# New tables of step places for a token tower followed by attention and MLP on one core

## What is computed

```
x = embed[tokens] + PE
for i in range(2):
    h = ln(x);  q, k, v = h@wq, h@wk/4, h@wv             # 8 heads of 16
    k, v = causal_conv(basis, k), causal_conv(basis, v)  # along the 256 positions
    Z = v (x) k;  g = relu(Z.gate_k + gate_b)**2 + 1e-5
    o = q . cumsum(g*Z) / (cumsum(g) + 1e-5);  o = o / max(|o|, 1e-5)
    x = x + o@wo;   x = x + gelu(ln(x)@ff1)@ff2
h = ln(x)@out_k + out_b                                   # 256 wide
h = h + attn(layernorm(h))    # 16 heads of 64: q (k^T v) / 8, then W_o; no softmax
h = h + mlp(layernorm(h))     # (silu(x@gate) * (x@up)) @ down, hidden 768, int8-valued weights / 127
```

## Time and profile before

| | |
|---|---|
| median of the runs | 1988.42 us |
| the profiled execution, its own time | 1988.27 us, 2.2 us of it outside the span |
| its span, first to last instruction | 1986.1 us |
| mean granted TensorE clock | 0.982 |
| PE busy | 1850.2 us (93%), 17146 matmuls |
| DVE busy | 1165.6 us (59%), 3019 instructions |
| ACT busy | 733.4 us (37%) |
| POOL busy | 439.4 us (22%), 391 instructions |

### The profile page before, as it was taken

How to read it: one execution, slowest core, us unless ns; L and a number is a source line. 1 busy time by engine, 2 the same in 40 slices (tenths; PEclk the granted TensorE clock), 3 DMA queues, 4 the chain that set the end, 5 groups by cost and what they waited for, 6 DMA issues and landing times.

```text
span 1986.1 us, 41766 instructions
## 1 busy us (share of the span) xinstructions
PE 1850.2 (93%) x17146; PEld 1588.0 (80%) x17146; DVE 1165.6 (59%) x3019; ACT 733.4 (37%) x1444; POOL 439.4 (22%) x391
## 2 busy tenths in 40 slices
...
GB/s 94 5 12 18 18 17 18 16 19 16 18 17 16 15 5 9 18 86 80 17 22 1 22 22 22 1 22 22 22 1 22 22 22 1 22 22 22 1 22 22
DMA packets 29211, 42.38 MB, mean 21 GB/s; under 512 B 5856, under 2 KB 22624, under 8 KB 29024
## 3 DMA queue, kind: packets, MB, share of 16 engines
...
q0 software_dynamic: 2048, 4.20, 0.8%
...
...
## 4 chain that ended last, share of the span: by engine, by line
PE 73%; DVE 17%; issue 4%; DMA 3%; POOL 2%; ACT 1%; SPq 1%; another core or an unknown queue 0%; DVEq 0%; POOLq 0%; ACTq 0%
PE ps L1406 11%; PE ps L1407 10%; PE ps L1408 10%; PE ps L806 3%; PE ps L1008 3%; PE ps L1456 3%; PE ps L1472 3%; DVE bxn L1271 3%; PE ps L887 3%; PE ps L807 3%; PE ps L808 3%; PE ps L959 3%; PE ps L937 2%; DVE bstats L1255 2%; DMA h<-h_rows 2%
## 5 line engine op out<-in xcount | busy, mean ns | idle before, releaser
L1245 POOL TENSOR_TENSOR hids_low<-hid,hids_high 128x512 fp32r<-128x512 f32 x96 | 137.6, 1440 | 611.0 <-ACT hids_high L1392 611.0
L512 POOL TENSOR_TENSOR rstd<-var,minus_half 128x4 f32<-128x4 f32 x80 | 82.5, 1032 | 564.5 <-DVE var L599 564.4
L757 ACT ACTIVATE xn<-x,shift,rstd 128x128 f32<-128x128 f32 x320 | 130.3, 482 | 133.6 <-DVE shift L604 133.6
L676 DVE TENSOR_TENSOR att<-ps,causal 128x512 f32<-128x512 f32 x256 | 158.6, 681 | 18.1 <-PE ps L937 18.0
L1406 PE MATMUL ps<-r_high,wq_high 128*128 128x256 f32 x512 | 147.4, 288 | 0.7 <-issue 0.7
L1407 PE MATMUL ps<-r_low,wq_high 128*128 128x256 f32 x512 | 144.9, 283 | 0.0
L1408 PE MATMUL ps<-r_high,wq_low 128*128 128x256 f32 x512 | 144.8, 283 | 0.0
L1386 ACT ACTIVATE silu<-ps 128x512 f32<-128x512 f32 x96 | 57.4, 598 | 226.5 <-DVE hid L1321 159.9
L1008 PE MATMUL ps<-w_f,wide 128*128 128x128 f32 x1024 | 130.1, 278 | 0.2 <-ACT wide L801 0.2
L1008 PEld LDWEIGHTS ps<-w_f,wide 128*128 128x128 f32 x1024 | 120.8, 192 | 6.0 <-issue 5.0
L1308 DVE TENSOR_TENSOR m_low<-ps,m_high 128x512 fp32r<-128x512 f32 x32 | 22.1, 692 | 170.8 <-ACT m_high L1378 170.8
...
## 6 DMA issues: line engine op xcount, KB each, us to landing
...
emb<-in_embed,idx POOLq DMA_INDIRECT x64
...
```

The costliest lines, as they stand in the source:

```text
L512: pool.tensor_tensor(rstd[s][:], var[s][:], minus_half[:], ALU.pow)\
L676: dve.tensor_tensor(masked[:, :, PAIR * g:PAIR * g + PAIR, :], bank("qk", s, l, j, g, t)[:].rearrange("p (n r t) -> p n r t", n=2, r=PAIR) ...
L757: act.activation(xn[s][:, j, :], x[s][:, j, :], ACT.Identity, bias=shift[s][:, j:j + 1], scale=rstd[s][:, j:j + 1]).then_inc(xn_made[s].se ...
L1245: pool.tensor_tensor(hids[1][:, halves, :], hid[:, half, :], hids[0][:, halves, :].bitcast(F32), ALU.subtract).then_inc(hid_low[s].sem, 1)
```

## The change

Only the six tables differ. Every number in them is another one; no step is added or removed, no function is touched. The steps of an engine come in a new order at some places. What differs in a steady group, engine by engine:

| where | before | after |
|---|---|---|
| A, PE | turn(1) state(1) av av turn_v(0) av av | state(1) av av turn(1) turn_v(0) av av |
| A, PE | f1 unit(1) gate(0) f1 wo(1) | unit(1) gate(0) f1 wo(1) f1 |
| A, PE | f1 f1 f1 sum(0) f2 f1 | f1 f1 sum(0) f1 f2 f1 |
| A, PE | f2 f2 unit(0) kv kv | f2 unit(0) f2 kv kv |
| A, PE | turn(0) conv conv wo(0) turn_v(1) q(1) | wo(0) turn(0) conv conv q(1) turn_v(1) |
| A, DVE | shift(2) shift(0) chain(0) low(2) | shift(2) chain(0) low(2) shift(0) |
| A, POOL | pow(1) bias(1) bias(2) gather gather gather bias(0) | bias(0) gather pow(1) gather gather bias(1) |
| A, POOL | pow(3) embed gather bias(3) pow(2) pow(0) | embed pow(3) pow(2) pow(0) bias(2) bias(3) gather |
| B, PE | keys keys t1 r t1 | keys keys r t1 t1 |
| B, PE | gate gate gate up gate up up gate gate up gram | gate gate up up gate up up gate gate gate gram |
| B, DVE | hid0 b_stats hid1 b_xn rows_low hid2 gram_low hid3 | hid0 b_stats b_xn hid1 rows_low hid2 hid3 gram_low |
| B, POOL | b_pow rows_high hid_low0 hid_low1 | hid_low0 b_pow rows_high hid_low1 |

(The number in brackets is the layer norm or layer that the step belongs to; steps that stand together belong to different groups.) Between the phases the first load of a weight piece stands two stores earlier on SP, and one `w_low` stands ahead of the second `b_stats` instead of behind it. At the start `kv_add` stands ahead of `kv_scale` on DVE.

```diff
-PLACES_A = [("embed", 0, 0, 750), ("stats", 0, 0, 601), ("pow", 0, 0, 868), ("shift", 0, 0, 710), ("xn", 0, 0, 874),
+PLACES_A = [("embed", 0, 0, 680), ("stats", 0, 0, 811), ("pow", 0, 0, 892), ("shift", 0, 0, 890), ("xn", 0, 0, 911),
...
-            ("chain", 0, 0, 1714), ("unit", 0, 0, 1687), ("unit_out", 0, 0, 1814), ("wo", 0, 0, 1835),
+            ("chain", 0, 0, 1874), ("unit", 0, 0, 1829), ("unit_out", 0, 0, 1912), ("wo", 0, 0, 1885),
...
-            ("turn", 2, 0, 2674), ("high", 2, 0, 2834), ("low", 2, 0, 2801), ("bias", 2, 0, 3261), ("q", 1, 0, 2849),
+            ("turn", 2, 0, 2751), ("high", 2, 0, 2901), ("low", 2, 0, 2886), ("bias", 2, 0, 2929), ("q", 1, 0, 2908),
...
-STARTS_A = [504, 1507, 2511, 3512, 4514, 5516, 6520, 7521, 8522, 9524, 10529, 11530, 12531, 13532, 14535, 15535]
+STARTS_A = [511, 1513, 2515, 3517, 4518, 5520, 6521, 7525, 8527, 9528, 10530, 11531, 12536, 13537, 14539, 15543]
-PLACES_B = [("b_load", 0, 0, 200), ("b_stats", 0, 0, 498), ("b_pow", 0, 0, 618), ("b_xn", 0, 0, 568),
+PLACES_B = [("b_load", 0, 0, 311), ("b_stats", 0, 0, 649), ("b_pow", 0, 0, 959), ("b_xn", 0, 0, 800),
...
-            ("b_up", 0, 0, 1569), ("silu", 0, 0, 1409), ("hid", 0, 0, 1470), ("hid_high", 0, 0, 1593),
-            ("hid_low", 0, 0, 2009), ("b_gate", 1, 0, 1393), ("b_up", 1, 0, 1657), ("silu", 1, 0, 1471),
-            ("hid", 1, 0, 1807), ("hid_high", 1, 0, 1924), ("hid_low", 1, 0, 2025), ("b_gate", 2, 0, 1552),
+            ("b_up", 0, 0, 1575), ("silu", 0, 0, 1862), ("hid", 0, 0, 1728), ("hid_high", 0, 0, 1951),
+            ("hid_low", 0, 0, 1655), ("b_gate", 1, 0, 1507), ("b_up", 1, 0, 1584), ("silu", 1, 0, 1881),
+            ("hid", 1, 0, 2085), ("hid_high", 1, 0, 2037), ("hid_low", 1, 0, 2256), ("b_gate", 2, 0, 1929),
...
-PREPARE = [("w_load", 0, 18419), ("w_high", 0, 18243), ("w_low", 0, 18125), ("w_load", 1, 18430),
+PREPARE = [("w_load", 0, 16744), ("w_high", 0, 18151), ("w_low", 0, 18518), ("w_load", 1, 17044),
...
-            ("kv_bias", 0, -6554), ("kv_scale", 0, -6440), ("kv_high", 0, -4902), ("kv_add", 0, -6139),
+            ("kv_bias", 0, -8184), ("kv_scale", 0, -4119), ("kv_high", 0, -3642), ("kv_add", 0, -6556),
```

114 lines of the change are left out of this document (72 added, 42 removed).

## The result

The changed kernel has a median of 1960.85 us (1958.46 to 1963.87) against 1988.60 us for the kernel before on the same chip: ratio 0.986, 95% interval 0.9842 to 0.9877, **27.8 us faster**. The forecast was 16.9 us faster. Repeated on the chip of the last experiments it took 1959.55 us, ratio 0.984 (0.983 to 0.986). The profiled execution has a span of 1958.3 us instead of 1986.1, at a mean granted clock of 0.984.

The account below looks back on a forecast made before the run. PE, nearly full in both phases, was taken as the bound, so only its idle time and order costs could be won. Terms -14.3 - 3.1 + 2 - 2.1 + 0.6 = -16.9 us gave 1971 us (chance 0.43), range 1950 to 1986.

Parts of the forecast that it names:

- no hold in A: Rival: in A, holding `chain` costs nothing (`bias(2)` comes after it, or the removed waits are larger); 1952 us, chance 0.20.
- the hold: A: `bias(2)` and `bias(3)` on POOL hold `chain` on DVE, so `unit(0)` waits 1.5 us a group.
- `gram`, minus 14.3: B: `xns_low` beats `hid_low1` to the port by 0.12 us, ending `gram`'s wait; 15 groups times 0.95 us.
- `hid_low0` is over before `b_pow` is ready: B, POOL: the `hid_low0` moved ahead of `b_pow` ends before `b_pow` is ready; no cost was counted.
- two bank claims: B, PE: `gate5` now needs `hid1`, second-half `gram` needs `hid2`; both done more than 0.5 us early.
- `keys` and `r`, minus 3.1: B, PE: three instead of four excursions into 64-wide shapes a group; 15 times 0.2 us gained.
- A, plus 0.15 a group: A: -2.5 us of waits against 0.3, 0.15, 0.7 and 1.5 of new costs; 13 groups, plus 2 us.
- `embed` is done before the gate operations: A: `embed` on POOL no longer meets the gate operations on DVE, so `state`'s wait for the gated keys goes.
- the query halves 0.15: A: with `turn_v(1)` behind `q(1)`, the query halves come about 0.15 us after PE needs them.
- `pow` as a holder: Rival: `pow` on POOL holds DVE too, so `chain` starts 0.4 us later in A; 1976 us, chance 0.06.
- The start, plus 0.6: Start: `kv_add` ahead of `kv_scale` starts the scalings and what follows 0.6 us later; bounds 0 and 2.
- Between the phases, minus 2.1: Crossing from A to B: earlier weight load gains 1.5 us, first `b_pow` ahead of `w_low` 0.6; bounds 0 and minus 4.

Follow-up runs that it names:

- run 3: The changed kernel with `hid1` put back ahead of `b_xn` in B (one key); 1979.68 us, ratio 0.9944 to the kernel before.
- run 1: The kernel before with two moves in B alone: `hid1` behind `b_xn`, `hid_low0` ahead of `b_pow`; 1978.44 us, ratio 0.9937.
- Run 5: The kernel before with four keys of B moved: `hid1` behind `b_xn`, `hid_low0` ahead of `b_pow`, `r` behind the second `keys`, `b_up0` ahead of `b_gate2`; 1972.75 us.
- run 2: The kernel before with one move in B: `r` behind the second `keys`, ahead of `t1`; 1986.06 us, ratio 0.9987.
- run 4: The changed kernel with one more wait on POOL: `bias(2)` of a group waits for `chain(0)` of the next; 1941.33 us, ratio 0.9746.
- Run 6: The kernel before with the gathers of A moved away from `av`, and first loads of the fourth group with them, on POOL alone; 1984.51 us, ratio 0.9965.
- run 7: The changed kernel with three of a group's four gathers moved on POOL, right behind `embed`, beside `av`; 1979.69 us, ratio 0.995.

## Why the prediction was right, and where it was not

The time fell in the range (1950 to 1986), 10 us under the forecast and 2 us under that case's own range (1963 to 1979): it lies between the forecast and the rival "no hold in A" (1952), although the hold is there. The total hides how far the terms were off. In differences of the profiled executions, B was forecast at minus 17.4 us and came to minus 23.5, A at plus 2 and came to minus 1.5 (over ten groups), the crossing at minus 2.1 and came to plus 0.7, the start at plus 0.6 and came to minus 3.5. By its steps:

**`gram`, minus 14.3: right in mechanism, by a margin that no plan should rest on.** I had 0.12 us, it is 0.05. The size was near: 17.1 us when undone (run 3), 12.5 us when done alone (run 1). Two things were wrong inside it. The wait in the earlier trace rows of 1.05 us understates the loss, as a wait is counted from the modelled end of the matmul before and `gram` then starts slowly: 0.22 us from its first matmul (1571.80 in the earlier trace rows) to its second, where the changed kernel has 0.12. And "`hid_low0` is over before `b_pow` is ready" left out `bvar`, which comes first; run 1 shows it held by 0.43 us. What pays for this in the change is the order of `b_gate` and `b_up`, which I had passed over as two bank claims: with `b_up0` third, not fourth, `hid0` comes one pair earlier. Run 5 closes the sum: race, early `b_up0` and `r` give a period of 64.8 to 65.1 against 66.2. The Trainium skill ("SBUF — State Buffer", section "Who interferes with whom") says that `tensor_scalar` can enter a mode in which it contends even with one SBUF input; `bvar` agrees with it, 0.60 against 0.17 us.

**`keys` and `r`, minus 3.1: right, as far as one can tell** (run 2: 2.6, interval 0.6 to 4.8).

**A, plus 0.15 a group: the hold right, `embed` wrong.** Measured minus 0.15 in the mean: minus 0.4 in six groups, plus 0.1 to 0.3 in four. Where all went as planned the sum is 0.55 us off, and no run says in which term. "`embed` is done before the gate operations" failed: `embed` starts within 0.3 us of `gk` (the rows of 418.93 and 470.08), and where it is first it costs some 0.5 us, which the sum had at nothing. Of its terms, `unit` waits 1.5 us (1.52 in the row above, cured by run 4), `wo` 0.7 (0.61), the query halves 0.15 (0.18 at L937), the wait of `av` for `state_low` is gone from the steady groups, and that of `state` for `gk` from six of ten. Two terms of the opposite sign nearly cancel, which is why the large one was invisible in the total and worth 20 us when taken out: the rival "no hold in A" is what run 4 makes true, 1.7 us a group where `embed` doesn't disturb (1.4 in the mean) where I had priced 1.5. (The reading of the earlier trace rows had the longest hold of `floor` at 0.95 us; it is 0.99.)

**`pow` as a holder, by the rule of the Trainium skill ("SBUF — State Buffer"): refuted.** `chain` begins beside `pow` in 14 groups of the changed kernel and keeps 0.19 us an operation; its first operation reads PSUM, so the harder evidence is the gate operation of the earlier trace rows (L641, `gate` and `b_gate`, both in SBUF): it meets a `pow` 14 times in the changed kernel too, and takes 0.19 us each time.

**The start, plus 0.6: the step that failed.** It came out at minus 3.5 by the first marker. `kv_add` did cost its part (`kv_high` starts 1.2 us later, 0.6 of it from a load that lands later), but the gathers beside `av` had cost more, and I had not looked for gaps that end on no engine: `issue` and `remote`. The step that failed is the path: I had taken the start for a chain of weight preparation alone, and put the gathers, PE's late signals behind them and the lower clock that follows at nothing. Run 6 takes the gathers from the kernel before and gets 2.5 us of these 3.5 (3.3 of 4.2 against the means of the executions).

**Between the phases, minus 2.1: half right at best.** `b_pow` of the first group is back at 1.01 us (1.65 in the earlier trace rows) and the long wait of `b_turn` is 5.46 instead of 6.09, the 0.6 forecast. The 1.53 us of ACT for the weight piece are gone too, but PE is no earlier for it: the stretch to the first `gram` is the same with both orders within the play of the executions (174.0 to 175.3 us). What the changed kernel gains in the first period of B is 3.2 us: 0.6 of `b_turn` and 0.2 of `r`. The 1.35 us that the second `gram` waited before are gone too, but not by the race: run 3 undoes it, and its first period is 66.5 us all the same, while run 5, which wins it, has 70.7. These 1.35 us and 1 us more stay open.

**What stays open** is how gathers make PE late. DVE has nothing to do from 380.1 to 383.4 us of run 7, so it isn't DVE at the port, and it isn't any three gathers in a row. The Trainium skill ("Runtime: NRT & Kernel Launch", Instruction fetch mechanics) describes how an engine refills its instructions in blocks over a DMA queue, which could meet the gathers; but from 378 to 384 us of run 7 the trace shows no packet of the instruction queues while ACT stands, so the runs don't support it.
